# Cross-attention and expert FFN on one core: row maxima issued from the scalar queue, and a different order of scatter, context and prologue transfers

## What is computed

```python
# x, ctx: (8, 256, 256); 16 heads of depth 16; 8 experts, top 2, capacity 1024
q = heads(layernorm(x) @ Wq + bq); k = heads(ctx @ Wk + bk); v = heads(ctx @ Wv + bv)
attn = softmax(q k^T / sqrt(16) + mask * -1e9)
x = x + concat(attn v) @ Wo + bo

xn = layernorm(x); scores = softmax(xn @ w_gate); weights, idx = top_k(scores, 2)
exp_x[idx, pos] += xn[token]              # pos: the token's place in its expert's list
h = exp_x @ c_fc; a, g = split(h)         # 256 -> 768
exp_out = (silu(a) * g) @ c_proj          # 384 -> 256
x = x + sum over the two choices of exp_out[idx, pos] * weight
```

## Time and profile before

| what | value |
|---|---|
| median of 3 executions | 466.27 us (464.39 to 466.72) |
| the profiled execution's own time | 467.2 us |
| its span, first to last instruction | 465.4 us |
| mean granted TensorE clock | 0.895 of full |
| PE busy | 384.8 us (83%) |
| DVE, ACT, POOL busy | 250.1 (54%), 211.8 (46%), 165.3 us (36%) |
| chain that ended last | PE 60%, DMA 13%, DVE 8%, issue 6%, SP's queue 5%, ACT 4% |

### The profile page before, as it was taken

How to read it: one execution, slowest core, us unless ns; L and a number is a source line. 1 busy time by engine, 2 the same in 40 slices (tenths; PEclk the granted TensorE clock), 3 DMA queues, 4 the chain that set the end, 5 groups by cost and what they waited for, 6 DMA issues and landing times.

```text
span 465.4 us, 9282 instructions
## 1 busy us (share of the span) xinstructions
PE 384.8 (83%) x2713; PEld 296.4 (64%) x2714; DVE 250.1 (54%) x694; ACT 211.8 (46%) x340; POOL 165.3 (36%) x174
## 2 busy tenths in 40 slices
PE   4546695996979969896979677979999999999990
PEld 3424463664655646563544346869999999999980
DVE  4544664585977868686876545463333323332330
ACT  2512363564455554563444154634445445444540
POOL 5021042521556435535050404163233333333332
PEclk9969798898988989898785659799999999999997
DMA  5578478392882928539060249534433234324440
GB/s 168 151 158 167 132 171 185 105 199 88 166 236 74 225 103 167 144 117 196 3 212 28 90 174 282 115 76 64 69 59 52 46 62 68 56 43 66 65 57 4
DMA packets 67514, 54.02 MB, mean 116 GB/s; under 512 B 11898, under 2 KB 64394, under 8 KB 67466
## 3 DMA queue, kind: packets, MB, share of 16 engines
q1 hardware_dynamic: 60076, 44.82, 40.0%
q0 software_dynamic: 7008, 8.43, 10.7%
q10 hardware_dynamic: 400, 0.40, 0.3%
HBM read 32.89 MB, written 21.18 MB: 116 GB/s over the span
## 4 chain that ended last, share of the span: by engine, by line
PE 60%; DMA 13%; DVE 8%; issue 6%; SPq 5%; ACT 4%; POOL 2%; ACTq 0%; POOLq 0%; DVEq 0%
PE bank L979 21%; PE bank L990 10%; PE bank L830 7%; DMA wf<-NMT 6%; PE bank L934 6%; PE bank L905 4%; PE bank L918 3%; PE bank L866 2%; DVE NEG L1107 2%; PE bank L839 2%; SPq L414 2%; SPq L429 2%; DMA qparts_d<-QP 2%; DMA kparts_d<-KP 2%; PE bank L959 2%
## 5 line engine op out<-in xcount | busy, mean ns | idle before, releaser
L1107 DVE TENSOR_REDUCE NEG<-bank 128x2 f32<-128x512 f32 x128 | 85.7, 684 | 51.6 <-PE bank L905 48.7
L979 PEld LDWEIGHTS bank<-CX,KS 128*128 128x128 f32 x912 | 109.1, 194 | 5.9 <-issue 3.8
L979 PE MATMUL bank<-CX,KS 128*128 128x128 f32 x912 | 109.8, 278 | 2.9 <-issue 2.8
L728 ACT ACTIVATE PR<-bank 128x512 f32<-128x512 f32 x128 | 73.4, 590 | 71.1 <-PE bank L918 70.1
L635 POOL DMA_INDIRECT out<-CTt,GG x38 | 58.9, 1550 | 101.3 <-DMA out<-CTt,GG 81.1
L763 ACT ACTIVATE KS<-wf 128x1536 f32 x40 | 59.2, 1483 | 47.1 <-PE bank L979 29.6
L905 PE MATMUL bank<-KS,wf 99*128 99x256 bf16 x224 | 45.7, 290 | 23.6 <-DVE NEG L1107 15.7
L1339 DVE COPY CX<-bank 128x256 f32<-128x256 f32 x39 | 16.5, 424 | 77.9 <-PE bank L959 59.3
L990 PE MATMUL bank<-wp,QF 128*128 x228 | 57.1, 388 | 0.8 <-DVE CTt L1353 0.8
L918 PE MATMUL bank<-wf,KS 102*128 102x256 bf16 x224 | 46.6, 291 | 9.6 <-DMA wf<-NMT 8.8
L572 POOL DMA_INDIRECT slots<-R,slot x32 | 32.2, 1005 | 61.5 <-DVE slot L1213 50.8
(11 more groups left out here) (170 smaller groups left out, 465.4 us busy)
## 6 DMA issues: line engine op xcount, KB each, us to landing
wf<-in_L_ffn_c_fc SPq DMA_DIRECT2D x8, 768.0 KB
XG<-slots SPq DMA_DIRECT2D x40, 128.0 KB
slots<-pad_row SPq DMA_DIRECT2D x8, 387.0 KB
kparts_d<-KP SPq DMA_DIRECT2D x8, 384.0 KB, 2.5
KS<-kparts_d SPq DMA_DIRECT2D x8, 384.0 KB
KS<-kparts_d SPq DMA_DIRECT2D x24, 128.0 KB
qparts_d<-QP SPq DMA_DIRECT2D x8, 384.0 KB, 3.1
wp<-in_L_ffn_c_proj SPq DMA_DIRECT2D x8, 384.0 KB
```

The costliest lines, as they stand in the source:

```text
L728: act.activation(PR[:, s % NPROB, :], STB[s % 2][:], ACT.Exp).then_inc(exp_done, 1)
L979: ins = pe.matmul(bank[2 + 2 * u + g][:, c * P:(c + 1) * P], UP[u][:, (k * 2 + g) * FF + c * P:(k * 2 + g) * FF + (c + 1) * P], XTG[:, u, ...
L1107: dve.tensor_reduce(NEG[:, n % 2, t, 2 * hp:2 * hp + 2], MXB[m % 2][:].rearrange("p (i s) -> p i s", i=2), AX.X, ALU.max, negate=True).the ...
```

## The change

The transfers of the maxima leave SP's stream and are issued by ScalarE on its own queue, one in each of three successive units (`max_row`). NM0 stands one unit earlier. SP's other transfers are reordered: contexts, the rows of `X`, and in batch 1 the parts. Batch 2's projection starts three units later, batch 1's one unit later. On GpSimd the scatter stands ahead of `layernorm2` in every pass.

```diff
@@ AT
-    "second K of the first": 2, "second Q of the first": 8, "start of 1": 6, "lead": 7,
-    "NM0": 11, "NM1": 2, ...
+    "second K of the first": 2, "second Q of the first": 8, "start of 1": 7, "lead": 7, "lead of 2": 4,
+    "NM0": 10, "NM1": 2, ...
@@ start_unit(n)
-    return UNITS * -2 + n * AT["start of 1"] if n < 2 else UNITS * (n - 2) - AT["lead"]
+    if n < 2:
+        return UNITS * -2 + n * AT["start of 1"]
+    return UNITS * (n - 2) - (AT["lead of 2"] if n == 2 else AT["lead"])
@@ sync
             sp.dma_start(wv[:], ...).then_inc(wv_in, 16)
+            load_rows(2)
             sp.wait_ge(qs_ones, 1)
...
             for it in ITERATIONS[:-1]:
-                if 3 <= it + 3 < B:
-                    load_context(it + 3)
-                if 0 <= it < B:
-                    max_rows(it, 1)
...
                     write_parts(n, KP, kp_ready, kd_out, kparts_d)
-                    if n < 2:
+                    if n == 0:
                         read_rows(n, KS[:, n % 3], ROWS3, 0, MATCH_K, kd_out, kparts_d)
+                    if n == 1:
+                        load_rows(3)
+                        load_context(2)
                     write_parts(n, QP, qp_ready, qd_out, qparts_d)
-                    if n >= 2:
+                    if n >= 1:
                         read_rows(n, KS[:, n % 3], ROWS3, 0, MATCH_K, kd_out, kparts_d)
                     read_rows(n, query_rows(n), 0, ROWS3, MATCH_Q, qd_out, qparts_d)
-                    if n == 0:
-                        load_rows(2)
-                        load_context(2)
-                    if n == 1:
-                        for m in range(3, B):
-                            load_rows(m)
...
                     sp.dma_start(out_t[it - 1], ...)
+                if 3 <= it + 4 < B:
+                    load_context(it + 4)
                 if 0 <= it < B:
                     if it < E - LATE:
                         load_up(it)
...
-                if 0 <= it + 1 < B:
-                    max_rows(it + 1, 0)
                 if it == -1:
                     load_rest()
+                    for m in range(4, B):
+                        load_rows(m)
@@ gpsimd
-                if it >= B - 2:
+                if 0 <= it - 2:
                     scatter(it - 2)
                 if 0 <= it - 1:
                     layernorm2(it - 1)
-                if 2 <= it < B - 2:
-                    scatter(it - 2)
@@ scalar
+            def max_row(n, half, j):
+                act.wait_ge(nmt_ready[half], n + 1)
+                if n >= 3:
+                    act.wait_ge(st_ready, UNITS * (n - 2))
+                act.dma_start(query_rows(n)[R_MAX + j:R_MAX + j + 1, 8 * half:8 * half + 8, :],
+                              NMT[8 * j:8 * j + 8, half, :]).then_inc(nm_in[half], 16)
...
                         if kind in ("CT", "XT", "K", "Q", "V", "NM0", "NM1", "X2"):
                             evacuate(kind, n)
+                    if AT["NM0"] <= u < AT["NM0"] + 3 and 0 <= it + 1 < B:
+                        max_row(it + 1, 0, u - AT["NM0"])
+                    if AT["NM1"] <= u < AT["NM1"] + 3 and 0 <= it < B:
+                        max_row(it, 1, u - AT["NM1"])
```

More of the change, by code:

```diff
@@ L76 @@
     "CT": 0, "K": 1, "XT": 5, "Q": 7, "second K": 9, "second Q": 10,
-    "second K of the first": 2, "second Q of the first": 8, "start of 1": 6, "lead": 7,
-    "NM0": 11, "NM1": 2, "PF": 3, "V": 4, "WO": 6, "X2": 12, "LG": 13, "CNT": 1, "BO": 12,
+    "second K of the first": 2, "second Q of the first": 8, "start of 1": 7, "lead": 7, "lead of 2": 4,
+    "NM0": 10, "NM1": 2, "PF": 3, "V": 4, "WO": 6, "X2": 12, "LG": 13, "CNT": 1, "BO": 12,
     "values": 5,
```

## The result

The changed kernel takes 463.93 us (median of 20 executions, 458.67 to 470.23) beside 467.16 us for the kernel before on the same chip (20 executions): a ratio of 0.991, interval 0.988 to 0.994. It is faster by 0.9%, 3 to 4 us, where 16 us were forecast, and 463.93 lies above the range's upper end of 461. (The ratio leaves out executions over 1.5% above the kernel's fastest, five of this one's 20, so it is not the quotient of the medians.)

What follows compares the result with a forecast made beforehand. TensorE was taken to stall at pass boundaries for half 0's maxima, queued behind SP's weights, then run at half clock. -6.0 + 0.5 - 14 - 8.2 + 9.8 + 1.8 = -16.1 from 467.2, median 0.9 lower: 450.2 us, range 439 to 461.

Steps and rivals of the forecast that it cites:

- Part 5: GpSimd's scatter ahead of layernorm2: scales come later, R meets the bias and ends later in passes 2 to 5; +1.8 us.
- the pair of pass 6: Bias on GpSimd beside R on VectorE in the earlier trace: R took 1.68 us in place of 0.73.
- The upper if the idle TensorE loses its clock: The scatter move's upper bound, 6 us, holds if TensorE, idle while R is late, drops its clock.
- Parts 2 to 4: Boundary stalls for maxima go (-14), clock holds before query projections (-8.2), six ScalarE issues a pass delay exponentials (+9.8).
- Part 3: Query projection at five boundaries runs at full clock without the stall, 1.99 in place of 3.62 us; -8.2 us.
- Part 1: Prologue: VectorE's 6.06 us wait for batch 3's X goes, -6.0 us; batch 2's later query projection costs 0.5.
- Rival 1: ScalarE's own queue doesn't help: the maxima still wait for all that SP issued before; about 459 us, chance 0.15.
- Rival 4: Only the prologue counts: next batch's key and query reads become late at each boundary; about 456 us, chance 0.17.
- Rivals 2 and 3: Issues not hidden make ScalarE the bound, 470.6 us (0.06); stalls go and ScalarE has slack, 439.6 us (0.13).
- The promised signs: Trace observations listed beforehand as showing the forecast right, or wrong, such as a 0.50 clock in units 12 to 15.

Runs made afterwards that it cites:

- the first comparison: The change (0.991) beside the changed kernel with GpSimd's layernorm2 ahead of the scatter again in passes 2 to 5 (0.967), on two chips.
- the one on a single chip: The change run a second time (0.986) beside the changed kernel with layernorm2 ahead of the scatter again in passes 2 to 5 (0.975), on the same chip.
- the change again: The changed kernel, unaltered, run a second time on another chip: 463.88 us, ratio 0.986 to the kernel before.
- layernorm2 first: The changed kernel with GpSimd's layernorm2 ahead of the scatter again in passes 2 to 5: 452.06 us (0.967), and on another chip 458.12 us (0.975).
- Before + ScalarE issues: The kernel before with only the maxima's six transfers on ScalarE's queue and NM0 one unit earlier: 455.18 us, ratio 0.976.
- Holding the bias: The changed kernel with GpSimd's bias addition, and KREST behind it, held until VectorE has written both pieces of R: 461.07 us (0.978), again 457.67 us (0.971).
- before + ScalarE issues + scatter first: The kernel before with ScalarE's issue of the maxima and the scatter ahead of layernorm2, without the new prologue and context order: 466.91 us, ratio 0.989.
- layernorm2, bias, scatter: The changed kernel with GpSimd's order in passes 2 to 5 turned to layernorm2, then bias, then scatter: 464.29 us, ratio 0.989.

## Why the prediction was wrong, step by step

**Part 5, the scatter ahead of layernorm2 (+1.8, bounds 0 and 6), is the step that failed.** By ratios it costs 0.024 (11 us) in the first comparison, across two chips, 0.011 (5 us) in the one on a single chip, and 0.013 (6 us) without the prologue, across two chips again: 5 to 11 us, where 1.8 was put in the sum and the upper bound was 6. With the old order, the rest of the change brings 0.033 (15.4 us) in the first comparison, where parts 1 to 4 add up to 17.9, so part 5 is 9 of the 12 us missing. On the single chip it brings 0.025 (12 us), so there these parts fall 6 us short and part 5 only 3.5; what they lack there isn't explained.

Three things in part 5's working were wrong, and a fourth is missing. The runs don't say how the 5 to 11 us divide among them.

- The collision was priced by the pair of pass 6 in the earlier trace rows, `R` 1.68 us beside the bias. In passes 2 to 4 another GpSimd instruction, `KREST`, follows the bias at once, so both pieces are blocked, and `R` takes 2.52. I had put a neighbour's price on a place with another queue behind it. This is the first profile; in the change again the collision is absent from passes 2 and 3, and the passes are as long.
- I took 0.3 us of each lateness as visible, on the ground that ScalarE is 1.1 us late there already. In the first profile TensorE waits 2.83 and 2.55 us for `R` in passes 2 and 3, beside 0.77 and 0.90 with layernorm2 first. About 2 us of each are visible.
- "The upper if the idle TensorE loses its clock" was a side remark, and it came true. Behind the wait for `R` the clock of passes 3 and 4 falls in the change, and it doesn't in the kernels with the wait repaired. The text named this as a sign of being wrong ("a granted clock of 0.50 in units 12 to 15"), but gave it no share of the sum.
- A pause of TensorE beside the scatter's issues, 1.7 to 2.9 us in each of passes 2 to 4 of the change again, stands in no part of the prediction. Its cause is open (last section).

**Parts 2 to 4 (-14 - 8.2 + 9.8 = -12.4)** were right as a sum, when the kernel has nothing else late. Before + ScalarE issues gives -12.8 us by the medians and -11 by the ratio. In the change itself the stalls are gone as forecast but for the first boundary: 22.5 us from unit 15 to unit 0 have become 10.2. The exponential behind `NMT` comes late about as worked out. ScalarE and its queue, after, pass 2:

```profile
123.12 0.36 ACT L679 ACTIVATE NMT<-bank 24x256 bf16<-24x256 bf16 x1
123.50 0.64 ACTq L709 DMA_DIRECT2D wf<-NMT  x1
124.24 0.60 ACT L723 ACTIVATE PR<-bank 128x512 f32<-128x512 f32 x1 [0.77 <-ACT NMT L679]
124.32 0.63 ACTq L709 DMA_DIRECT2D wf<-NMT  x1
125.05 0.60 ACT L723 ACTIVATE PR<-bank 128x512 f32<-128x512 f32 x1 [0.21 <-issue]
```

The first issue leaves the engine 0.77 us idle; the second lies under an exponential. Part 3's 8.2 us were realized only in part in the change. The query projections of passes 1 to 5 took 3.6, 3.1, 3.6, 3.1 and 3.2 us before and take 3.1, 1.9, 1.9, 2.2 and 2.0, which is 5.7 us less; but the clock is lost again ahead of the boundaries, and between 120 and 205 us it is the 0.92 of before. In the kernel with ScalarE's issue alone it is 1.00.

**Part 1 (-6.0 + 0.5)** was too large. The wait of 6.06 us for `X` is gone, but pass 0's first logits start at 50.3, not 47. What was late next was not 1 us but more: batch 2's key projection, moved into unit 13, runs at half clock:

```profile
45.27 3.74 PE L829 MATMUL bank<-CTt,wk 128*128 128x256 f32 x8 [0.29 <-ACT CTt L655]
```

And the 0.5 us for batch 2's later queries were too few. Its reads are issued from 65.9 us on and land when TensorE has waited 4.55 us. The chain, after:

```profile
67.61 8.64 DMA wf<-qparts_d
```

Layernorm2 first, which has the new prologue, beside before + ScalarE issues, which has not, gives the price on one chip: first logits at 49.0 and 53.9 us, pass 0 longer by 1.6, and 452.06 against 455.18 in all, so -3.1 (-4.3 by the ratios) in place of -5.5.

**The rivals.** Rival 1 had the number nearest to the result (459), but not its mechanism: the transfers of maxima are no longer waited for. Rival 4's mechanism, the key and query reads become late, holds at one boundary of six. Rivals 2 and 3 fall: exponentials aren't spaced by issues, and ScalarE had no slack to hide all of them. No rival had the true one, which was a term of mine at its wrong size.

**Own queue or not.** Between 123 and 126.9 us ScalarE issues three transfers, and no packet of its queue runs. DMA view of after for that stretch (queue: packets, MB, share of 16 engines):

```profile
q1 hardware_dynamic: 896, 1.03, 83.7%
q0 software_dynamic: 157, 0.42, 27.7%
...
wf<-NMT ACTq DMA_DIRECT2D x3, 4.0 KB
```

For over 4 us the maxima wait while SP's earlier transfers run, as they did before. From 128 to 129 us 30 of their packets run, but beside 301 of SP's queue, so they don't wait for all of it. The Trainium skill's page "DMA: Bandwidth & Descriptors" has two rules on this, named in the prediction. In the first 4 us "Issuing engines are not separate DMA queues" is nearer to the trace than the packet-by-packet turns of "Queues, rings and completion order"; from 128 us on it is the other way round. The gain came all the same. The transfers are issued at 123.50, 124.32 and 126.46, all ahead of a boundary at 130.8. In the kernel before SP issued them from 129.91 to 132.01, behind the expert weights, for a boundary at 136.8.

**The promised signs**: waits of L917 for the maxima 1.5 us in two places (right); boundaries about 1 us (right at five of six); query projection 2.0 us at full clock (right at passes 2 and 3, 1.89 us; 3.10 at pass 1, 2.15 at pass 4); first logits near 47 (wrong, 50.3); VectorE without a wait for `X` (right); `R` 1.68 us in passes 2 to 5 (wrong, 2.52 in 2 to 4); half clock in units 12 to 15 (the sign of being wrong, seen in passes 3 and 4).

## What to carry to other kernels

A stall hides all the lateness that lies in it. When a change takes the stall away, each other part of the same change must be priced against the schedule without it: the scatter's move cost 0 us beside SP's stall and 5 to 11 without. Of a VectorE operation that GpSimd can block, look at every GpSimd instruction that will stand beside it, not only at the first. Of the two cures found here, the better one to take is the old order of layernorm2 and scatter, with all the rest of the change: 0.967 and 0.975 of the time before, in place of 0.991 and 0.986. Holding the bias is as good in the whole time where it was measured beside it (0.971), but slower in passes 2 to 4.

## What the runs showed of the hardware that was not expected

**A pause of TensorE that is not explained.** In the change as run again, and in each of the other kernels on its chip and on that of "before + ScalarE issues + scatter first" that have the scatter ahead of layernorm2, the context's transposes in unit 11 of passes 2 to 4 deliver 1.7 to 3.6 us late. ScalarE, the change again, passes 1 to 4:

```profile
92.56 0.60 ACT L655 ACTIVATE CTt<-bank 128x512 f32<-128x512 f32 x1 [0.99 <-PE bank L808]
...
119.89 0.60 ACT L655 ACTIVATE CTt<-bank 128x512 f32<-128x512 f32 x1 [2.69 <-remote]
...
148.70 0.60 ACT L655 ACTIVATE CTt<-bank 128x512 f32<-128x512 f32 x1 [3.08 <-remote]
...
176.82 0.60 ACT L655 ACTIVATE CTt<-bank 128x512 f32<-128x512 f32 x1 [3.86 <-remote]
```

"remote" means that the profile finds no instruction or transfer that released the wait; by their records the transposes of pass 2 end at 118.16, 1.73 us ahead of this wait's end. The waits in passes 2 to 4 are 1.7 to 2.9 us over the 0.99 of pass 1, which has no scatter. The four scatter issues run at these times (from 144.24 to 149.19 in pass 3). With layernorm2 first, on the same chip, the wait is 0.99 in all four passes; in layernorm2, bias, scatter the pause stands where the scatter then is, at the boundary. The two kernels with the scatter first and SP's issue show 0.99 as well. In the first profile of the change, on another chip, the same place shows 0.99 and the collision at `R` instead: there `R` is 14.0 us busy, here 8.6, with the same ratio within the intervals. So the pause goes with the scatter's issues, and it may be another part of the scatter's cost; but bias held has it too (2.72 to 3.19 us) and is as fast in all as layernorm2 first, which hasn't, though 2.7 us slower in passes 2 to 4. What it is, why only some chips show it, and how much of the time it takes stays open. It wasn't tried to move the transposes away from the issues.

How the cost of the scatter's move divides between `R`'s length, the pause and the half-clock stretches wasn't separated either. What is shown is that the kernel is faster with the move undone, in each of the three comparisons, and that holding the bias behind `R` shortens the whole time as much on one chip.
